# Gated cross-attention block with an autocorrelation stage: two of four context transforms made from the other two by copies with exchanged partition halves

## The reference, cut to what matters

```python
qf = jnp.fft.fft(q, axis=2)
kf = jnp.fft.fft(k, axis=2)
corr = jnp.fft.ifft(qf * jnp.conj(kf), axis=2).real
topk = int(C * np.log(L))                    # 9 lags
w, idx = jax.lax.top_k(corr.transpose(0, 1, 3, 2), topk)
w = jax.nn.softmax(w, axis=-1)
for i in range(topk):
    g = jnp.minimum(idx[:, :, None, :, i] + pos, L - 1)
    out = out + w[:, :, None, :, i] * jnp.take_along_axis(v, g, axis=2)
...
x = x + jnp.tanh(g_xattn[0]) * _L0_xattn_ref(_layernorm(x), ctx, ctx)
x = x + jnp.tanh(g_ffn[0]) * _L0_ffn_ref(_layernorm(x), ...)     # router, top 2 of 8
x = x + jnp.tanh(g_xattn[1]) * _L1_xattn_ref(_layernorm(x), ctx, mask, ...)
x = x + jnp.tanh(g_ffn[1]) * _L1_ffn_ref(_layernorm(x), ...)
```

## Time and profile before

| | |
|---|---|
| time, median of 3 runs (lowest, highest) | 886.33 us (886.28, 888.25) |
| span of the profiled execution | 882.5 us |
| first matmul of the second block of work | 194.0 us |
| TensorE / VectorE / ScalarE / GpSimd busy over the span | 94% / 69% / 47% / 47% |
| chain that ended last, TensorE's share | 71% |

### The profile page before, as it was taken

The page is one execution under the profiler, slowest core; times in us unless marked ns, Lnnn a source line. Parts: engine busy times, 40 slices in busy tenths (PEclk is TensorE's granted clock), DMA queues, the critical chain, the costliest instruction groups (busy, mean ns, idle before and its releaser), DMA issues.

```text
span 882.5 us, 15501 instructions
## 1 busy us (share of the span) xinstructions
PE 830.6 (94%) x4592; PEld 684.3 (78%) x4592; DVE 605.8 (69%) x1710; ACT 416.3 (47%) x1271; POOL 411.8 (47%) x484
## 2 busy tenths in 40 slices
PE   4888889769999999999999999999999999999897
PEld 3555556438888888888888888888888888888786
DVE  5789999633666666676666666666766667666995
ACT  3344444323654455455545545554555455445431
POOL 2566776643553255336435532553363355335532
PEclk9899999889999999999999999999999999999999
DMA  7401000010110011001101100110012010100011
GB/s 262 147 24 30 31 24 13 0 49 24 39 58 25 1 49 61 13 0 48 71 0 48 48 24 0 48 59 12 0 48 71 0 48 24 48 1 13 0 38 59
DMA packets 16947, 34.34 MB, mean 39 GB/s; under 512 B 2320, under 2 KB 2448, under 8 KB 16656
## 3 DMA queue, kind: packets, MB, share of 16 engines
q1 hardware_dynamic: 16912, 33.91, 11.9%
HBM read 31.80 MB, written 2.10 MB: 38 GB/s over the span
## 4 chain that ended last, share of the span: by engine, by line
PE 71%; DVE 3%; issue 2%; POOL 1%; ACT 0%; DVEq 0%; POOLq 0%
PE bank L1122 19%; PE bank L1124 18%; PE bank L1123 18%; PE bank L1210 5%; PE bank L1136 4%; PE bank L1163 3%; PE bank L1138 2%; DVE score L1316 1%; PE bank L1218 1%; POOL rq L1005 1%; PE bank L1226 0%; POOL rk L1001 0%; ACT prob L1050 0%; PE bank L1236 0%; POOL probn L994 0%
## 5 line engine op out<-in xcount | busy, mean ns | idle before, releaser
L994 POOL TENSOR_TENSOR probn<-prob,erec 128x512 f32<-128x512 f32 x64 | 66.8, 1043 | 252.0 <-PE bank L1163 222.4
L1077 ACT ACTIVATE qT_hi<-bank 128x512 fp32r<-128x512 f32 x64 | 38.3, 599 | 161.9 <-PE bank L1124 161.9
L1122 PE MATMUL bank<-nT_hi,wq_hi 128*128 128x512 f32 x256 | 105.2, 411 | 1.8 <-POOL ones L960 1.8
L1122 PE MATMUL bank<-wo_hi,oT_hi 128*128 128x512 f32 x256 | 105.0, 410 | 0.4 <-DVE wq_raw L1373 0.4
L1050 ACT ACTIVATE prob<-score,nmax 128x128 f32<-128x128 f32 x256 | 99.6, 402 | 9.9 <-DVE nmax L1321 9.8
L1124 PE MATMUL bank<-nT_hi,wq_lo 128*128 128x512 f32 x256 | 102.1, 399 | 0.0
L1123 PE MATMUL bank<-nT_lo,wq_hi 128*128 128x512 f32 x256 | 101.9, 398 | 0.0
L1124 PE MATMUL bank<-wo_hi,oT_lo 128*128 128x512 f32 x256 | 100.9, 394 | 0.0
L1123 PE MATMUL bank<-wo_lo,oT_hi 128*128 128x512 f32 x256 | 99.7, 389 | 0.0
L1005 POOL TENSOR_TENSOR rq<-qss,neghalf 128x4 f32<-128x4 f32 x64 | 65.1, 1017 | 50.3 <-DVE qss L1387 50.3
L1381 DVE TENSOR_SCALAR knat<-bank,rk 128x128 f32<-128x128 f32 x64 | 22.4, 350 | 95.4 <-POOL rk L1001 95.4
(11 more groups left out here) (192 smaller groups left out, 2191.8 us busy)
## 6 DMA issues: line engine op xcount, KB each, us to landing
wq_raw<-in_wq SPq DMA_DIRECT2D x32, 256.0 KB, 3.6
wo_raw<-in_wo SPq DMA_DIRECT2D x32, 256.0 KB, 3.0
wkv_raw<-in_wkv SPq DMA_DIRECT2D x8, 512.0 KB, 3.6
ctxn<-in_ctx_n SPq DMA_DIRECT2D x8, 256.0 KB, 2.7
ctxt<-in_ctx_t SPq DMA_DIRECT2D x8, 256.0 KB, 2.7
out<-wkv_raw SPq DMA_DIRECT2D x8, 256.0 KB, 2.0
xres<-in_x SPq DMA_DIRECT2D x1, 1280.0 KB, 11.3
wbase<-in_wbase SPq DMA_DIRECT2D x1, 1024.0 KB, 8.2
```

Source lines behind the costliest of these rows:

```text
L994: pool.tensor_tensor(probn[:], prob[:], erec[:].unsqueeze(2).broadcast_to([P, HG, P]), ALU.mult).then_inc(normed, 1)
L1077: act.activation(qT_hi[:, s % HG, first * P:(first + 4) * P], q_bank[:], ACT.Copy).then_inc(q_h, 1)
L1122: pe.matmul(out, l_hi, r_hi, start=start, stop=False)
```

## The change

Only transforms 0 (even, `V_EVEN`) and 2 (odd, `V_ODD`) are still matrix products: `ctx_transform(b, 0)` into `bank1` and `ctx_transform(b, 1)` into `bank2`. The swapped ones are made by ScalarE from the same bank: its lower 64 partitions go to the upper 64 of `kf`, and the upper to the lower, two instructions of 64 partitions. The last row now rides in row 0 of the even transform itself (`v_even[0, P - 1] += P`), and the inverse constants are adjusted (`crossed`, `c_inv1[0] = 0`). The constants are 11 in place of 12 matrices, and the high and low parts of the forward constants hold 2 in place of 4. A bank is now released when both of its copies are done, and the second transform waits only for the copies of the batch before.

```diff
                 def copy_ctx_dfts(b, which):
                     for i in which:
+                        half, of = P // 2, bank[1 + i // 2]
                         if i % 2 == 0:
                             need(act, o_prod, 4 * b + i - 2)
-                        need(act, k_fwd, 4 * b + i + 1)
-                        act.activation(kf[:, i, :], bank[1 + i % 2][:], ACT.Copy).then_inc(k_copied, 1)
+                            need(act, k_fwd, 2 * b + i // 2 + 1)
+                            act.activation(kf[:, i, :], of[:], ACT.Copy).then_inc(k_copied, 1)
+                        else:
+                            act.activation(kf[0:half, i, :], of[half:P, :], ACT.Copy)
+                            act.activation(kf[half:P, i, :], of[0:half, :], ACT.Copy).then_inc(k_copied, 1)
...
-                    need(pe, k_copied, 4 * b + i - 1)
-                    three_pass(bank[1 + i % 2][:], fwd_hi[:, i, :], fwd_lo[:, i, :], cx_hi[:], cx_lo[:],
+                    need(pe, k_copied, 4 * b - 2 + 2 * i)
+                    three_pass(bank[1 + i][:], fwd_hi[:, i, :], fwd_lo[:, i, :], cx_hi[:], cx_lo[:],
                                True, True).then_inc(k_fwd, 1)
...
                     if on(b + 1):
                         ctx_transform(b + 1, 0)
-                        ctx_transform(b + 1, 1)
...
                     if on(b + 1):
-                        ctx_transform(b + 1, 2)
-                        ctx_transform(b + 1, 3)
+                        ctx_transform(b + 1, 1)
...
-                for i in range(4):
+                for i in range(2):
                     ctx_transform(0, i)
...
-    m = [fwd.T, fwd_sw.T, less_last_row(odd_fwd).T, less_last_row(odd_fwd_sw).T, odd_fwd.T, inv1, inv2,
-         inv1 / 2, even_inv2, odd_inv1, odd_inv2, np.eye(P)]
+    v_even = fwd.copy()
+    v_even[0, P - 1] += P
+    v_odd = odd_fwd.copy()
+    v_odd[:, P - 1] -= odd_fwd.sum(1)
+    c_inv1 = inv1.copy()
+    c_inv1[0] = 0
+    m = [fwd.T, v_even.T, v_odd.T, odd_fwd.T, c_inv1, inv2, inv1 / 2, -inv2 / 2, odd_inv1, odd_inv2, np.eye(P)]
```

More of the change, by code:

```diff
@@ L37 @@
 RMS_EPS = 1e-5
-(K_FWD, K_FWD_SW, V_ODD, V_ODD_SW, W_ODD, C_INV1, C_INV2,
- E_INV1, E_INV2, O_INV1, O_INV2, IDENT) = range(12)
-N_DFT = 12
+(FWD, V_EVEN, V_ODD, W_ODD, C_INV1, C_INV2,
+ E_INV1, E_INV2, O_INV1, O_INV2, IDENT) = range(11)
+N_DFT = 11
 def need(eng, sem, value, hold=False):
@@ L151, in phase_a @@
         dft = sb(st, "dft", [P, N_DFT, P])
-        fwd_hi = sb(st, "fwd_hi", [P, 4, P], F32R)
-        fwd_lo = sb(st, "fwd_lo", [P, 4, P], F32R)
+        fwd_hi = sb(st, "fwd_hi", [P, 2, P], F32R)
+        fwd_lo = sb(st, "fwd_lo", [P, 2, P], F32R)
         inv_hi = sb(st, "inv_hi", [P, 4, P], F32R)
@@ L401, in high_ctx @@
                     need(act, ld_c, 16 * b + 16)
-                    need(act, k_fwd, 4 * b)
+                    need(act, k_fwd, 2 * b)
                     act.activation(cx_hi[:], ctxn[:], ACT.Copy).then_inc(cx_h, 1)
@@ L490, in q_transform @@
                     need(pe, e_lag, CH * b)
-                    pe.matmul(bank[0][:], dft[:, K_FWD, :], nx[:], start=True, stop=True).then_inc(q_fwd, 1)
+                    pe.matmul(bank[0][:], dft[:, FWD, :], nx[:], start=True, stop=True).then_inc(q_fwd, 1)
                 def ctx_transform(b, i):
@@ L542, in slot @@
                         need(pe, g_norm, b - 2)
-                        need(pe, k_copied, 4 * b + 3 if not isinstance(b, int) else min(4 * b + 3, 4 * B))
+                        need(pe, k_copied, 4 * b + 2 if not isinstance(b, int) else min(4 * b + 2, 4 * B))
                         if closing(b):
@@ L567, in slot @@
                         need(pe, f_added, b)
-                        pe.matmul(bank[3][:], dft[:, K_FWD, :], wT[:], start=True, stop=True).then_inc(w_fwd, 1)
+                        pe.matmul(bank[3][:], dft[:, FWD, :], wT[:], start=True, stop=True).then_inc(w_fwd, 1)
                         pe.matmul(bank[4][:], dft[:, W_ODD, :], wT[:], start=True, stop=True).then_inc(w_fwd, 1)
@@ L737, in _ @@
                 dve.wait_ge(ld_dft, 16)
-                for i, (lo, hi, m) in enumerate(((fwd_lo, fwd_hi, K_FWD), (inv_lo, inv_hi, E_INV1))):
+                for i, (lo, hi, m, n) in enumerate(((fwd_lo, fwd_hi, V_EVEN, 2), (inv_lo, inv_hi, E_INV1, 4))):
                     dve.wait_ge(dft_h, i + 1)
-                    dve.tensor_tensor(lo[:], dft[:, m:m + 4, :], hi[:].bitcast(F32), ALU.subtract).then_inc(dft_l, 1)
+                    dve.tensor_tensor(lo[:], dft[:, m:m + n, :], hi[:].bitcast(F32), ALU.subtract).then_inc(dft_l, 1)
                 dve.tensor_copy(ident[:], dft[:, IDENT, :]).then_inc(ident_done, 1)
@@ L1432, in dft_constants @@
     fwd = np.where(is_im, -np.sin(ph), np.cos(ph))
-    fwd_sw = np.where(is_im, np.cos(ph), -np.sin(ph))
     weight = np.where((f == 0) | (f == P // 2), 1.0, 2.0)[:, None]
+    crossed = ((f != 0) & (f != P // 2))[:, None]
     inv1 = weight * np.cos(ph) / P
-    inv2 = np.where(is_im, -1, 1) * weight * np.sin(ph) / P
+    inv2 = np.where(crossed, np.where(is_im, -1, 1) * weight * np.sin(ph) / P, 0.0)
     odd = np.concatenate([np.arange(P // 2)] * 2)
@@ L1440, in dft_constants @@
     odd_fwd = np.where(is_im, -np.sin(ph), np.cos(ph))
-    odd_fwd_sw = np.where(is_im, np.cos(ph), -np.sin(ph))
     odd_inv1 = np.cos(ph) / P
     odd_inv2 = np.where(is_im, 1, -1) * np.sin(ph) / P
[L1445 to L1455, removed]
-    m = [fwd.T, fwd_sw.T, less_last_row(odd_fwd).T, less_last_row(odd_fwd_sw).T, odd_fwd.T, inv1, inv2,
-         inv1 / 2, even_inv2, odd_inv1, odd_inv2, np.eye(P)]
+    v_even = fwd.copy()
[5 more added lines that the diff above has]
+    m = [fwd.T, v_even.T, v_odd.T, odd_fwd.T, c_inv1, inv2, inv1 / 2, -inv2 / 2, odd_inv1, odd_inv2, np.eye(P)]
     return np.ascontiguousarray(np.stack(m, axis=1).astype(np.float32))
```

2 lines of the change are left out of this document (1 added, 1 removed).

## The result

The changed kernel takes 893.36 us (median of 4 runs, 891.87 to 894.59) against 886.31 for the kernel before (4 runs, 885.43 to 888.25): ratio 1.0084, 95% interval 1.0064 to 1.0103. In two later measurements of the same program the medians are 891.02 and 891.89 against 885.63 and 884.92, ratios 1.0065 [1.0049, 1.0080] and 1.0068 [1.0049, 1.0087]. So it is slower, by 5.4 to 7.1 us, where 888.3 was forecast; all three medians lie above the range (890.8), the nearest by 0.2. One execution of e8 (931.40 us at a mean granted clock of 0.845) stands apart from its other five and is left out of its ratio; all others are used. In the executions on record whose span is given too, the time is 1.7 to 2.1 us longer than the span, not some 4 us; the 3.8 us between 886.33 and 882.5 are those and the difference between two executions.

A forecast was written before the change was run, and what follows sets the result against it. The prediction took VectorE, with short waits on ScalarE and GpSimd, to bound the changed first stage. Start -0.3, slot 0 +0.3, slot 1 -0.45 and slots 2 to 6 +2.4 sum to +1.95 on 886.33: 888.3 us, range 885.0 to 890.8.

The forecast's parts named there:

- What bounds the stage: First stage, eight batches: VectorE sets the pace, with short waits on ScalarE and GpSimd; removed transforms worth nothing in slots 2 to 6.
- TensorE's work comes through in full: Rival: all 11.2 us of the removed TensorE matmuls in the first stage are gained, giving 875.1 us; chance 0.04.
- ScalarE's price: Swapped copies in the first stage: each extra half copy costs 0.48 us from start to start.
- Half copies do not overlap: Rival, ScalarE's swapped copies: each starts when the one before is done, 0.60; 0.36 more per slot, 890.1 us; chance 0.12.
- What carries it to the end: Slots 2 to 6: ScalarE's delay reaches VectorE through op_hi and GpSimd's op_lo, full 0.48 a slot, +2.4, lower bound 1.5.
- Clock: Rival: TensorE's clock falls in the loop too; 0.25 more per slot, slot 0 at its upper bound, 890.1 us; chance 0.18.
- Slot 0: First slot: lag weights turned sooner, -0.45, but correlations perhaps at the lower clock; +0.3 taken, bounds -0.45 and +1.3.
- Slot 1: VectorE's wait of 0.93 us for the correlations shrinks as one transform ahead goes: -0.45, bounds -0.9 and 0.
- Start: Before slot 0: the second product can start at 12.75 instead of 13.06, -0.3; smaller constants taken as 0.
- Second stage: After the eight batches: untouched, only starts later or earlier, and lasts the same 688.5 us.
- the signs that I named: In the trace: half copies 0.48 apart, second product 0.04 behind second half, period 20.55, no slot 1 wait, second stage 688.5.

The follow-up runs named there:

- e8: The kernel before, with the first op_hi moved ahead of the straight copy and the second product behind the residual addition: 879.99 us, ratio 0.9939.
- e1: The changed kernel with each swapped copy made as one plain 128x512 copy, without exchange of the halves: 885.71 us, ratio 1.0005.
- e2: The changed kernel with each of the two remaining transforms computed twice, so TensorE has its old load: 890.45 us, ratio 1.0061.
- e12: The changed kernel with each of the two transforms computed twice, measured again: 891.03 us, ratio 1.0060.
- e9: The changed kernel with a twelfth, unused matrix of zeros in the constants, so their load is 768 KB as before: 891.55 us, ratio 1.0083.
- e4: The changed kernel with the two halves copied straight, lower to lower and upper to upper, without the exchange: 888.88 us (1 run).
- e5: The changed kernel with the first of four op_hi moved ahead of the straight copy on ScalarE: 886.54 us, ratio 1.0012.
- e10: The changed kernel with VectorE's second product made later, behind the residual addition, and ScalarE's order kept: 888.02 us, ratio 1.0034.
- after: The changed kernel itself, in its first measurement and profiled trace, against the kernel before: 893.36 us, ratio 1.0084.
- e11: The changed kernel measured again, nothing else changed: 891.89 us, ratio 1.0068.
- e0: The changed kernel measured once more, nothing else changed: 891.02 us, ratio 1.0065.
- e6: The changed kernel with both moves, first op_hi ahead of the straight copy and second product behind the residual addition: 881.40 us, ratio 0.9957.

## Why the prediction was wrong

The forecast of 888.3 had the right sign, the right engines and too small a sum. The chances gave slower than 0.3% only 0.36. The step that failed is ScalarE's price, 0.48 us for a half copy that cost 0.87. Step by step:

1. **What bounds the stage: right.** TensorE's 48 matmuls are worth nothing (e1, ratio 1.0005). "TensorE's work comes through in full" is out.
2. **ScalarE's price: the step that failed.** The instruction was costed at 0.48 us, the spacing of like instructions; it was 0.48 plus three holds of 0.13, 0.87 in all. "Half copies do not overlap" was a rival at 0.12, priced 0.84 per slot, and it is what happened: e2, e12 and e9 have 0.82 to 0.88 in slots 3 to 6, so the five slots cost 5 x 0.83 = 4.2 where +2.4 was forecast. It was a rival of this very mechanism, and I gave it little although no row that I had read of the kernel before had a change of starting partition, so that the rows could say nothing for the overlap. e4 shows the condition: it is the start, not the count.
3. **What carries it to the end: right in kind.** The slot grew by 0.83 of the 0.87, so nearly the full delay came through, and the tiny copy behind op_lo is one way for it: e5 takes that hold away, and the slot is back at 20.11. It is not the only one, as e10 shows (0.28 a slot at the product).
4. **Clock: in the loop it came in part, at the end it was not thought of.** Forecast 0.25 a slot if it fell; measured 0.25 in e1, 0.27 to 0.3 in two slots of after. It was treated as one rival against the other, and the two came together in the first trace. As a sum, 888.3 + 1.8 + 0.5 would have been 890.6 before slot 0. The forecast had nothing for the end of the stage, where the fall cost 2.5 us in three traces of the changed kernel.
5. **Slot 0: under-sized.** +0.3 with a bound of +1.3; the traces of the changed kernel show +2.63, +1.14 and +2.63. I had let only the correlations run at the lower clock. In after the whole stretch from 22 to 30 us had it (0.50 against 0.87), and with it the matmuls that VectorE's products there wait for (L571, 2.07 us). The traces line up in part: +2.63 where the clock of that stretch was 0.50 to 0.53 (after, e11, e5), +0.7 to +1.1 where it was 0.71 to 0.84 (e0, e4, e9, e10, e6, e8), both with lighter load and, in e8, without. But e1, with the lighter load and whole copies, has 0.81 and +0.06, and the old load with half copies 0.79 and +0.28 (e2) or 0.64 and +0.80 (e12). So the slot is longest where the clock was 0.50 to 0.53; what the rest of it is made of stays open.
6. **Slot 1: gain larger than forecast (0.92 for 0.45), and lost again in slot 2.** I had checked only that the wait would go, not what the instruction behind it would then run into. Slots 1 and 2 together, less slot 2's 0.83 for the half copies, are +0.10 in after (-0.92 + 1.85 - 0.83) where -0.45 was forecast. It isn't one stall only: in e5 ntop is free again (0.17 us), yet slot 2 is still 0.94 longer, because there another small VectorE instruction (rwn, 8 elements long) comes 0.12 us behind the start of two op_lo, takes 1.19 us instead of 0.23, and the normalising of n2 starts only at 73.50:

```profile
72.27 2.51 POOL L387 TENSOR_TENSOR op_lo<-op,op_hi 128x512 fp32r<-128x512 f32 x2
72.39 1.19 DVE L693 TENSOR_SCALAR rwn<-rw,rrec 128x8 f32<-128x8 f32 x1
```

7. **Start: forecast -0.3, measured nothing.** Here too the half copies come 0.61 apart and not 0.48, so the second product starts 5.21 to 5.24 us behind the first matmul in e0, e9 and after, where it was 5.27 before (13.06 - 7.79). That is the failed step once more. Late constants can add up to 1.3 us by chance, as in after; e0, e9, e10, e5 and e11 have -0.23 to +0.06.
8. **Second stage: right.** 688.5 before, 688.8 after.

Of the signs that I named, the two halves are not 0.48 but 0.61 apart; the product starts 0.03 behind the second half's end (134.87 to 134.90), as said; the period is 20.92 and not 20.55; the search of slot 2 waits no longer. In the sum, slots 2 to 6 at 0.83 in place of 0.48 are 1.75 us more, +0.10 in place of -0.45 for slots 1 and 2 is 0.55 more, and a start that gains nothing 0.3 more: +4.55 in place of +1.95. The executions at the higher clock lie 4.3 to 5.0 us above the later medians of before. The low-clock stretches make the rest, 3.4 us more in the other executions, and so the medians of 891.0, 891.9 and 893.4: a mix in the first two, and in the third only executions at 0.977 and 0.979.

## What to carry to other kernels

An exchange of partition halves by copies isn't one more instruction of the same price: each change of the starting partition cost ScalarE the overlap with its neighbour, 0.13 us a time, and the instructions behind it pay that as well. Before taking a delay as absorbed, or a removed wait as gained, look at the small instruction behind it: here a copy of two elements (0.16 to 1.05 us) and a multiplication of four (0.17 to 1.31 us), held by a GpSimd instruction, decided much of what came through. And where the engine with 94% does not end the waits, ask what the order on the engine that does end them leaves free: two moves of instructions gave 5.6 us (885.63 to 879.99), and the 48 matmuls nothing. An experiment can also bring a cost of its own: the doubled transforms added 1.2 us ahead of slot 0, which the subtraction of medians would have put down to the half copies.

## What the runs showed of the hardware that I had not expected

- ScalarE: a 64x512 copy from a bank takes 0.59 us like a 128x512 one; start to start it is 0.48 to 0.50 with the same starting partition and 0.59 to 0.62 when that changes, on either side.
- Three small VectorE instructions, 2 to 8 elements long and 0.16 to 0.28 us when free, took 1.05, 1.19 and 1.31 us beside GpSimd's subtractions over 512: what is held can be far smaller than what holds it.
- TensorE's clock: in one and the same program the stretch from 22 to 30 us was granted 0.50 in one execution and 0.84 in another, and the slot was 1.5 us longer in the first. At the end of the stage six microseconds of the same matmuls had 0.56 in two of its executions and 1.00 in e9's, 2.5 us apart.
- The first load of the constants: with 704 KB it was there by 7.58 us in one execution and at 9.05 in another of the same program.
